# Setup of a four-layer convolution kernel: layer 2's adapters contracted over 8 ranks x 16 adapters, shared adapter in four row groups, four subtractions on GpSimd

## The reference

```python
A_eff = jnp.einsum('bn,nri->bri', gate, lora_A)
B_eff = jnp.einsum('bn,nor->bor', gate, lora_B)
Ax = jnp.einsum('bri,bti->btr', A_eff, x_flat)
delta_flat = jnp.einsum('bor,btr->bto', B_eff, Ax)
Ax_s = jnp.einsum('ri,bti->btr', lora_A_shared, x_flat)
delta_flat = delta_flat + jnp.einsum('or,btr->bto', lora_B_shared, Ax_s)
```

## Time and profile before

| what | value |
|---|---|
| median of 3 runs | 1207.51 us (1206.16 to 1208.16) |
| the profiled execution's own time | 1208.1 us |
| its span | 1206.3 us |
| mean granted clock of PE | 0.996 |
| busy PE, DVE, ACT, POOL | 97%, 43%, 29%, 45% |
| first matmul of the main program | 79.80 us from the span's start |

### The profile page before, as it was taken

How to read it: one execution, slowest core, us unless ns; L and a number is a source line. 1 busy time by engine, 2 the same in 40 slices (tenths; PEclk the granted TensorE clock), 3 DMA queues, 4 the chain that set the end, 5 groups by cost and what they waited for, 6 DMA issues and landing times.

```text
span 1206.3 us, 38332 instructions
## 1 busy us (share of the span) xinstructions
PE 1172.3 (97%) x17688; PEld 686.7 (57%) x17688; DVE 520.3 (43%) x1012; ACT 349.8 (29%) x634; POOL 541.3 (45%) x411
## 2 busy tenths in 40 slices
PE   5899999999999999999999999999999999999997
PEld 4345565555565555655555556555566565565565
DVE  6863443443343434343444343444343344434343
ACT  2253233233222223123322222323222223313221
POOL 4657524555435436444155553355354541654300
PEclk9899999999999999999999999999999999999999
DMA  5534100021313000002123000002112100001001
GB/s 151 231 137 173 40 2 2 2 63 71 142 60 118 2 2 2 2 6 94 72 72 134 10 2 2 2 2 98 72 48 82 50 2 2 2 1 72 2 19 53
DMA packets 21567, 63.30 MB, mean 52 GB/s; under 512 B 4672, under 2 KB 5376, under 8 KB 17184
## 3 DMA queue, kind: packets, MB, share of 16 engines
q1 hardware_dynamic: 19632, 60.13, 13.7%
q10 hardware_dynamic: 1776, 0.73, 0.3%
HBM read 43.02 MB, written 17.83 MB: 50 GB/s over the span
## 4 chain that ended last, share of the span: by engine, by line
PE 88%; DVE 4%; issue 0%; DMA 0%; ACT 0%; DVEq 0%
PE bank_b L1326 28%; PE bank_a L119 14%; PE bank_a L106 11%; PE bank_b L106 11%; PE bank_b L89 9%; PE bank_a L1263 5%; PE bank_b L1284 3%; PE bank_a L77 3%; PE bank_b L1278 2%; PE bank_b L1338 2%; PE bank_b L1319 1%; DVE z L1169 1%; PE bank_b L1297 1%; PE bank_b L1307 1%; PE bank_b L1340 1%
## 5 line engine op out<-in xcount | busy, mean ns | idle before, releaser
L934 POOL TENSOR_TENSOR sum_v<-raw_v 128x768 f32<-128x768 f32 x30 | 55.3, 1844 | 552.8 <-ACT raw_v L993 552.8
L1326 PE MATMUL bank_b<-w_hi,y3t_hi 128*128 128x512 f32 x512 | 208.4, 407 | 0.0
L1326 PE MATMUL bank_b<-w_hi,y3t_lo 128*128 128x512 f32 x512 | 202.5, 395 | 0.0
L1326 PE MATMUL bank_b<-w_lo,y3t_hi 128*128 128x512 f32 x512 | 202.0, 394 | 0.0
L119 PE MATMUL bank_a<-y,w_down 64*32 64x512 f32 x3072 | 172.2, 590 | 0.0
L1119 DVE TENSOR_TENSOR x<-bank_b,x 128x512 f32<-128x512 f32 x96 | 66.4, 692 | 180.0 <-PE bank_b L1326 140.2
L986 ACT ACTIVATE y<-bank_a,cb,tab 128x512 f32<-128x512 f32 x64 | 49.6, 776 | 314.6 <-PE bank_a L119 309.2
L106 PE MATMUL bank_a<-y,wv 32*64 32x512 f32 (+2 forms) x3584 | 138.1, 476 | 0.8 <-issue 0.8
L106 PE MATMUL bank_b<-y,wv 32*64 32x512 f32 (+2 forms) x3584 | 137.2, 476 | 0.0
L1326 PEld LDWEIGHTS bank_b<-w_hi,y3t_hi 128*128 128x128 f32 x512 | 96.6, 189 | 35.1 <-issue 13.4
L89 PE MATMUL bank_b<-xs,cw 32*32 32x512 f32 x3072 | 111.9, 611 | 2.7 <-DVE var L553 1.9
(11 more groups left out here) (194 smaller groups left out, 1444.1 us busy)
## 6 DMA issues: line engine op xcount, KB each, us to landing
w_hi<-w_scratch SPq DMA_DIRECT2D x9, 1024.0 KB, 5.3
w_lo<-w_scratch SPq DMA_DIRECT2D x9, 1024.0 KB, 8.0
x_in<-in_x SPq DMA_DIRECT2D x32, 256.0 KB, 4.2
out_x<-out_tile SPq DMA_DIRECT2D x32, 256.0 KB, 2.3
w_raw<-in_w SPq DMA_DIRECT2D x3, 1024.0 KB, 6.4
w_scratch<-w_hi SPq DMA_DIRECT2D x3, 1024.0 KB, 4.2
w_scratch<-w_lo SPq DMA_DIRECT2D x3, 1024.0 KB, 7.1
w_raw<-w_scratch SPq DMA_DIRECT2D x2, 1024.0 KB, 9.9
```

The costliest lines, as they stand in the source:

```text
L934: ins = g_.tensor_tensor(dst[:, :, at:at + count].rearrange("p r k o -> p r (k o)"), src[:, :, 0:count].rearrange("p r k o -> p r (k o)"), ...
L1326: ins = pe.matmul(lin_ps[b][:], y3t[yi][:, k, P * b:P * (b + 1)], w[use(m) % 2][wi][:, k], start=(k == 0 and i == 0), stop=(k == KB - 1 an ...
```

## The change

- Each per-sample factor is laid out as 128 partitions = 8 ranks x 16 adapters, with four chunks of ranks. `gate_t` is 128 x 8, `delta` 128 x 8, and `gmat` one product of 8 x 8 elements. A chunk is one matmul with all 128 rows and 64 output partitions (8 blocks x 8 ranks); two chunks fill the two halves of a bank. There are 4 matmuls in place of 8 for each factor and nothing is accumulated. The scratch arrays have the order of the new layout, and the reloads gather each block from four chunks.
- The shared adapter's factors are loaded four times, onto four groups of 32 partitions; each of the four matmuls takes its own group. ACT issues eight loads in place of two.
- The `hi` parts of the five small factors move on ACT ahead of the `hi` parts of `b2`. The `lo` parts of `a1, r1, b1, a3` move from DVE to POOL, ahead of `blurred(1)`; that of `b3` stays.

```diff
@@ loads, ACT's queue
-                ("as2", as2[:], io["as2"]), ("bs2", bs2[:], io["bs2"]),
+                *(("as2", as2[R2 * p:R2 * (p + 1)], io["as2"]) for p in range(KB)),
+                *(("bs2", bs2[R2 * p:R2 * (p + 1)], io["bs2"]) for p in range(KB)),
@@ ACT
             evacuate_2(1)
+            for name, raw, hi, *_ in small:
+                act.wait_ge(loaded[name], 16 * (len(PASSES) if name == "b3" else 1))
+                a.activation(hi, raw, ACT.Copy).then_inc(small_hi, 1)
...
             ins.then_inc(down_ready, 1)
-            for name, raw, hi, *_ in small:
-                act.wait_ge(loaded[name], 16 * (len(PASSES) if name == "b3" else 1))
-                a.activation(hi, raw, ACT.Copy).then_inc(small_hi, 1)
@@ POOL
-            for kk in range(4):
-                g.tensor_tensor(gmat[:, kk], gate_t[:, kk].unsqueeze(2).broadcast_to((P, 8, R2)),
-                                delta[:].unsqueeze(1).broadcast_to((P, 8, R2)), ALU.mult).then_inc(gm_ready, 1)
+            g.tensor_tensor(gmat[:], gate_t[:].unsqueeze(2).broadcast_to((P, 8, 8)),
+                            delta[:].unsqueeze(1).broadcast_to((P, 8, 8)), ALU.mult).then_inc(gm_ready, 1)
...
             scaled_input(1)
+            for k, (*_, raw, hi, lo) in enumerate(small[:-1]):
+                pool.wait_ge(small_hi, k + 1)
+                g.tensor_tensor(lo, raw, hi.bitcast(F32), ALU.subtract).then_inc(small_lo, 1)
             blurred(1)
@@ DVE
-            for k, (*_, raw, hi, lo) in enumerate(small):
-                dve.wait_ge(small_hi, k + 1)
-                v.tensor_tensor(lo, raw, hi.bitcast(F32), ALU.subtract).then_inc(small_lo, 1)
+            *_, raw, hi, lo = small[-1]
+            dve.wait_ge(small_hi, len(small))
+            v.tensor_tensor(lo, raw, hi.bitcast(F32), ALU.subtract).then_inc(small_lo, 1)
@@ PE
             for p in range(KB):
-                pe.matmul(w2_ps[p][:], as2[:, p * P:(p + 1) * P], bs2[:], start=True, stop=True).then_inc(w2_done, 1)
+                rows = slice(R2 * p, R2 * (p + 1))
+                pe.matmul(w2_ps[p][:], as2[rows, p * P:(p + 1) * P], bs2[rows], start=True, stop=True).then_inc(w2_done, 1)
...
-                    for kk in range(4):
-                        last = pe.matmul(banks[h][:], g2[:, kk, h * P:(h + 1) * P], raw[:, kk],
-                                         start=(kk == 0), stop=(kk == 3))
+                    for c in range(2):
+                        last = pe.matmul(banks[h][P // 2 * c:P // 2 * (c + 1)], g2, raw[:, 2 * h + c], start=True, stop=True)
@@ SP, stores and reloads
-                    sp.dma_start(scratch[name][i, 4 * h:4 * h + 4].rearrange("b r n -> (b r) n"),
+                    sp.dma_start(scratch[name][i, 2 * h:2 * h + 2].rearrange("c b j n -> (c b j) n"),
...
-                                     scratch["a2"][i_a][2 * it + g]).then_inc(adapters_loaded, 16)
+                                     scratch["a2"][i_a][:, 2 * it + g]).then_inc(adapters_loaded, 16)
@@ host layout
-    a2 = i["L2_ffn_lora_A"].reshape(4, P, LEN).transpose(1, 0, 2)
+    a2 = i["L2_ffn_lora_A"].reshape(16, 4, 8, LEN).transpose(2, 0, 1, 3).reshape(P, 4, LEN)
```

More of the change, by code:

```diff
@@ L185, in setup_program @@
     b3 = sb("b3_raw", [len(PASSES) * E3 * R3, LEN])
-    as2 = sb("as2_raw", [R2, LEN])
-    bs2 = sb("bs2_raw", [R2, LEN])
+    as2 = sb("as2_raw", [P, LEN])
+    bs2 = sb("bs2_raw", [P, LEN])
     w2, w0_add = (sb(n, [P, KB, LEN]) for n in ("w2", "w0_add"))
-    gate_t = sb("gate_t", [P, 4, 8])
-    delta = sb("delta", [P, R2])
-    gmat = sb("gmat", [P, 4, 8, R2])
+    gate_t = sb("gate_t", [P, 8])
+    delta = sb("delta", [P, 8])
+    gmat = sb("gmat", [P, 8, 8])
     a2eff = [keep["w_sum"][:, 2 * i:2 * i + 2].bitcast(F32R) for i in range(2)]
@@ L697, in _ @@
             conv2_tiles(pe, bank_a, keep, 1).then_inc(keep["c2_done"], 1)
-            pe.wait_ge(loaded["as2"], 16)
-            pe.wait_ge(loaded["bs2"], 16)
+            pe.wait_ge(loaded["as2"], 16 * KB)
+            pe.wait_ge(loaded["bs2"], 16 * KB)
             pe.wait_ge(keep["y2_ends"], 1)
             for p in range(KB):
-                pe.matmul(w2_ps[p][:], as2[:, p * P:(p + 1) * P], bs2[:], start=True, stop=True).then_inc(w2_done, 1)
-            pe.wait_ge(gm_ready, 4)
+                rows = slice(R2 * p, R2 * (p + 1))
+                pe.matmul(w2_ps[p][:], as2[rows, p * P:(p + 1) * P], bs2[rows], start=True, stop=True).then_inc(w2_done, 1)
+            pe.wait_ge(gm_ready, 1)
             pe.wait_ge(loaded["a2"], 16)
             pe.wait_ge(loaded["b2"], 16)
-            g2 = gmat[:].rearrange("p k b r -> p k (b r)")
+            g2 = gmat[:].rearrange("p b j -> p (b j)")
             for banks, raw, done, added in ((b2_ps, b2, b2_done, 2), (a2_ps, a2, a2_done, KB)):
@@ L848, in load_adapters @@
                         sp.dma_start(keep["a2s"][rows, g].bitcast(F32),
-                                     scratch["a2"][i_a][2 * it + g]).then_inc(adapters_loaded, 16)
+                                     scratch["a2"][i_a][:, 2 * it + g]).then_inc(adapters_loaded, 16)
                         sp.dma_start(keep["b2s"][rows, g].bitcast(F32),
-                                     scratch["b2"][i_b][2 * it + g]).then_inc(adapters_loaded, 16)
+                                     scratch["b2"][i_b][:, 2 * it + g]).then_inc(adapters_loaded, 16)
             def load_raw(l):
@@ L1452, in build @@
             "w2": nc.dram_tensor("w2_scratch", [P, KB, LEN], F32).ap(),
-            "a2": nc.dram_tensor("a2_scratch", [2, 8, R2, LEN], F32).ap(),
-            "b2": nc.dram_tensor("b2_scratch", [2, 8, R2, LEN], F32).ap(),
+            "a2": nc.dram_tensor("a2_scratch", [2, 4, 8, R2 // 4, LEN], F32).ap(),
+            "b2": nc.dram_tensor("b2_scratch", [2, 4, 8, R2 // 4, LEN], F32).ap(),
         }
@@ L1498, in host_layout @@
     b0 = c(i["L0_ffn_Bf"].transpose(0, 2, 1)).reshape(2, P, LEN).transpose(1, 0, 2)
-    a2 = i["L2_ffn_lora_A"].reshape(4, P, LEN).transpose(1, 0, 2)
-    b2 = c(i["L2_ffn_lora_B"].transpose(0, 2, 1)).reshape(4, P, LEN).transpose(1, 0, 2)
+    a2 = i["L2_ffn_lora_A"].reshape(16, 4, 8, LEN).transpose(2, 0, 1, 3).reshape(P, 4, LEN)
+    b2 = i["L2_ffn_lora_B"].transpose(0, 2, 1).reshape(16, 4, 8, LEN).transpose(2, 0, 1, 3).reshape(P, 4, LEN)
     x = i["x"].reshape(GROUPS, ROWS, ROWS, CH, LEN).transpose(0, 1, 3, 2, 4).reshape(GROUPS, P, ROWS, LEN)
@@ L1521, in host_layout @@
         "a2": a2, "b2": b2,
-        "gate_t": np.repeat(i["L2_ffn_gate"].T, R2, axis=0).reshape(4, P, 8).transpose(1, 0, 2),
-        "delta": np.tile(np.eye(R2, dtype=np.float32), (ROWS, 1)),
+        "gate_t": np.tile(i["L2_ffn_gate"].T, (8, 1)),
+        "delta": np.repeat(np.eye(8, dtype=np.float32), 16, axis=0),
         "as2": i["L2_ffn_lora_A_shared"],
```

## The result

The changed kernel takes 1212.18 us (median of 6 runs, 1211.41 to 1213.36), the one before 1207.63 beside it (6 runs): a ratio of 1.0038, 95% interval 1.0024 to 1.0051. It is slower, by 0.4%. The profiled execution took 1212.36 us, its span is 1210.5 (before 1206.3, so 4.2 more), its mean granted clock 0.992 (before 0.996).

The account below looks back on a forecast made before the run. PE holds 88% of the chain of waits; the change touches only setup, where PE's matmuls and DVE's list end together. Main program 3.8 us earlier, 2.0 lost to PE's restart: -1.8 us, 1205.7 us, range 1202.8 to 1208.2.

Parts of the forecast that it names:

- the early part: Setup up to the `w2` additions: longer ACT queue, shorter `gmat`, earlier scales; additions at 53.0, 1.6 us earlier.
- the term of the column scales: Early setup on DVE: short instructions run while POOL waits for `ob`; scales ready near 33.8 instead of 36.76, 3.0 us earlier.
- Rival 2: Early setup: `ob` addition starts before DVE's three scalings, so no early gain; 2.2 gained, 2.0 lost, 1207.3 us; chance 0.17.
- The late part: Setup from the `w2` additions on: four DVE subtractions gone, blurs lengthen the late tables; main program at 76.0, 3.8 us earlier.
- the four row groups: Shared adapter's four matmuls on PE in setup: side by side they take 0.9 us instead of 3.69.
- the column halves: Per-sample matmuls on PE in setup: 3.6 us per factor if nothing overlaps, 1.8 in pairs; before 8.83 and 7.13.
- The restart: Main program's first convolution: after some 7 us of PE idling it runs at a low clock, 2.0 us lost, bounds 1.4 and 2.9.
- theory C: Stated after the measurement: eight matmuls fewer moved a PE code boundary into a transfer burst; the main program stalls near 125 us.
- Rival 4: Setup: POOL's subtractions and additions hold DVE ahead of the `w2` additions; main program at 80.8, 1210.5 us; chance 0.08.

Follow-up runs that it names:

- e1: Changed kernel with the shared adapter's eight loads issued on SyncE's queue behind `a1` and `b1` instead of ACT's: 1207.61 us, ratio 0.9998 to the kernel before.
- e9: Changed kernel with one more wait: POOL's additions of `ob` start only when DVE has the column scales: 1208.79 us, ratio 1.0012 to the kernel before.
- e3: Changed kernel with PE's last convolutions of the setup computed twice (48 more matmuls): 1209.32 us, ratio 1.0023 to the kernel before.
- e8: Changed kernel with only the per-sample adapters kept; shared factors loaded once, `hi` and `lo` parts back in place: 1211.17 us, ratio 1.0029 to the kernel before.
- e4: e1 with POOL's last blur waiting for DVE's late tables and the `lo` part of `b3` ahead of them: 1203.64 us, ratio 0.9972 to the kernel before.
- e5: Changed kernel with eight more matmuls on PE, in the idle time ahead of the last convolutions: 1210.30 us, ratio 1.0023 to the kernel before.
- e12: e3 with POOL's additions of `ob` also waiting for DVE's column scales: 1210.71 us, ratio 1.0019 to the kernel before.
- e7: e4 with the first half of the setup's last convolutions computed twice (24 more matmuls): 1202.27 us, ratio 0.9964 to the kernel before.

## Why the prediction was wrong

**The failing step is the early part**, the term of the column scales: 3.0 us earlier, with bounds of 0 and 3.0; measured, 3.2 us later (40.0 for 36.76). The prediction said: six more issues at 0.48 us, table load at 23.1, square root 0.65 us later, scales at 33.8, with 0.3 us to spare before POOL's additions. The queue grew by 4.2 us instead of 2.9 and the square root came 2.0 us later. The 0.48 is what most issues take, before as after (the kernel before issues its own `as2` and `bs2` at 0.45 each). What the price left out are the long ones. The kernel before has one in its list:

```profile
16.42 1.39 ACTq L298 DMA_DIRECT2D b_raw<-in_b  x1
```

The changed kernel has one like it at 16.58 and, its list being longer, another at 20.35, when the list before was already over (20.20). That is 0.75 us; the first two of the new issues take 0.59 and 0.71 (0.40 together), and the list starts 0.16 later. The 14 traces have 20 issues of over 1 us in this list, and each ends 0.3 to 0.4 us behind the end of a packet of kind "instruction" on q8 (in the changed kernel those that start at 16.67 and 20.22). That the packet is what holds the issue is not shown.

With the square root 2.0 us late, DVE's eight table instructions, which take 0.97 us when nothing holds them (32.36 to 33.33 in e1), began 0.14 us behind POOL's additions instead of ending 0.3 ahead of them. The scales came at 40.0 instead of 33.8, the `w2` additions at 58.25 instead of 53.0. Rival 2 had this mechanism, but priced it by before's scalings alone (2.4 us): it took the scales to be no later than before. When the race is lost at its first instruction, all eight table instructions stand under the additions, and the loss grows to 6.2 us.

e1 (the loads off ACT's queue) shows the whole chain, from the square root to the main program. e9 (the long queue, but the order set by a wait) and e3's run (the long queue, but `ob` late) give the scales back at 36.2 and 35.07; from there to the main program's start e3's run keeps 2.29 us and e9's 0.66. A margin of 0.3 us would have been luck even at the right price: POOL's start moved over 2.4 us with the landing of `ob`, and in e8, with the short queue, the additions still caught DVE's last three scalings.

**The late part held.** From the `w2` additions to the main program the forecast had 23.0 us; it was 21.9. The tables took 11.4 us (5.8 + 6.0 forecast), `b2`, `b3` and `a2` 1.3 + 0.7 + 1.3. `gmat` took 0.30 as estimated, the four row groups 1.14 (0.9), the column halves 3.21 and 1.94 (1.8 to 3.6). Three late tables took 1.74, 2.17 and 2.42 us, each to the end of a blur, where such instructions take 0.25 to 0.26 with POOL idle (e4). The Trainium skill's rule of "SBUF — State Buffer", section "Who interferes with whom" (a DVE instruction with two SBUF inputs that comes second blocks until GpSimd's has finished), agrees with that.

**The restart held**: 5.14 us against 3.40, 1.74 for the forecast 2.0, and e3 takes it away.

**One term was missing**: 2.08 us for a stall in the main program, by theory C for code that came late. The prediction put it at nothing, since the change touches none of the work there. That is true of the work and not of its place in the code. Without it the forecast for e1's case, -1.8, would have been near: e1 is at -1.25 just ahead of the stall, and ends level with before.

**Rival 4**, the one on the slower side, gave 1210.5 by another way (POOL holding DVE's tables and weight blocks ahead of the `w2` additions). That its 80.8 for the main start is near the 80.18 is luck: POOL held the column scales, and behind them ACT and PE came late (the second half of `w0` started at 42.35); DVE itself waited 4.00 us for PE's conv2 at 52.38.

## What to carry over

Price issues on a queue by the whole list with its long ones (before, eleven in the 6.58 us from 13.65 to 20.23, 0.60 each), not by the shortest of their kind. When a gain rests on winning a race by a fraction of a microsecond, compare that with how far a landing in it moves from run to run, and count the loss from the first instruction that loses. Work taken off an engine that is not what ends a block only lengthens its idling, and here that idling cost clock. When instructions are removed from a long unrolled program, look along all of it for new gaps that nothing in the program explains, beside full DMA engines, before a sum of terms is believed because it fits.

## What the runs showed that was not expected

- Removing 8 matmuls in the setup cost 2 us at 125 us in the main program, and adding 8 (e5) took it away: a 16 KB packet of kind "instruction" came at 123.9 us, at the end of a burst of transfers, instead of ahead of it. The same kind of gap stands in the kernel before, 0.83 us at 307.12. That these pieces are PE's code is inferred, not read from the trace: from the lengths of PE's list, from its 17672 matmuls and as many weight loads against 2054 instructions of DVE, ACT and POOL and 139 packets, and from the 140 packets of the two kernels with 48 matmuls more (e3, e12).
- DMA issues in ACT's list took from 0.39 to 2.43 us each (2.43 in e7), and the same issue 0.63 in one kernel and 1.41 in another. Those of over 1 us all go with one of the q8 packets; what makes them long is not shown.
